# Down products of fourteen of sixteen column groups, in sweeps 2 to 4, by seven half-width products

## The reference

```python
gate = einsum('th,nh->tn', xt, Wg)                # 4096 tokens, 512 -> 4096
up = einsum('th,nh->tn', xt, Wu)
inter = gelu(gate) * up
out = einsum('tn,hn->th', inter, Wd)              # 4096 -> 512
x = layernorm(x + out)
```

## Time and profile before

| | |
|---|---|
| median of 3 runs | 2691.85 us (2691.76 to 2693.28) |
| the profiled execution, its own time | 2691.47 us |
| its span, first to last instruction | 2689.7 us |
| PE busy | 98% of the span |
| PE weight loads | 80% |
| DVE, ACT, POOL busy | 58%, 41%, 31% |
| mean granted TensorE clock | 0.993 of full speed |

### The profile page before, as it was taken

One profiled execution on the slowest core, in us unless ns is written; L12 is line 12 of the kernel. 1 busy time (PEld: TensorE's weight loads), 2 busy tenths in 40 slices (PEclk: granted clock), 3 DMA queues, 4 the chain that ended last, 5 costly groups with the idle time before them and its releaser, 6 DMA issues.

```text
span 2689.7 us, 37714 instructions
## 1 busy us (share of the span) xinstructions
PE 2629.1 (98%) x13314; PEld 2147.7 (80%) x13314; DVE 1555.4 (58%) x3224; ACT 1103.2 (41%) x2518; POOL 824.0 (31%) x992
## 2 busy tenths in 40 slices
PE   7999999999789999999999999999999999999998
PEld 6787887778468888888888888888888888888886
DVE  5677777777789888876333333633333363333334
ACT  4666666666644544443222222322222232222221
POOL 1444444443634343434111111321111132111112
PEclk9999999999899999999999999999999999999999
DMA  8676876778465655565444333554344345433441
GB/s 247 182 186 172 220 210 172 189 193 228 110 245 212 226 213 208 196 264 232 169 174 188 162 141 142 207 206 172 142 185 167 141 158 229 169 141 141 180 172 48
DMA packets 143085, 493.52 MB, mean 183 GB/s; under 512 B 11568, under 2 KB 48560, under 8 KB 118320
## 3 DMA queue, kind: packets, MB, share of 16 engines
q1 hardware_dynamic: 142896, 491.11, 53.0%
HBM read 356.84 MB, written 134.22 MB: 183 GB/s over the span
## 4 chain that ended last, share of the span: by engine, by line
PE 71%; DVE 1%; DMA 1%; issue 1%; ACT 0%; POOL 0%; SPq 0%; POOLq 0%; DVEq 0%; ACTq 0%
PE bank L1034 23%; PE bank L1035 23%; PE bank L1036 23%; PE bank L451 0%; DMA scale<-down_scales 0%; DMA x1T_scratch<-x_late 0%; DVE bstats L1482 0%; PE bank L437 0%; DVE acc L1425 0%; ACT probs L559 0%; PE bank L461 0%; PE bank L418 0%; ACT bx_h L1165 0%; DVE bits L1385 0%; DVE y L704 0%
## 5 line engine op out<-in xcount | busy, mean ns | idle before, releaser
L1644 POOL TENSOR_TENSOR inter_l<-hid,inter_h 128x512 fp32r<-128x512 f32 x256 | 337.6, 1319 | 1362.0 <-ACT inter_h L1165 1362.0
L1425 DVE TENSOR_TENSOR acc<-acc,bank 128x512 f32<-128x512 f32 x512 | 349.9, 684 | 332.4 <-PE bank L1036 322.9
L1034 PE MATMUL bank<-wd,inter_h 128*128 128x512 f32 x1024 | 399.7, 390 | 6.3 <-DVE acc L1425 5.3
L1036 PE MATMUL bank<-wd,inter_l 128*128 128x512 f32 x1024 | 398.9, 390 | 0.0
L1035 PE MATMUL bank<-wd,inter_h 128*128 128x512 f32 x1024 | 398.9, 390 | 0.0
L739 POOL TENSOR_SCALAR probs<-probs,row_inv 128x128 f32<-128x128 f32 (+3 forms) x512 | 263.0, 533 | 366.2 <-DVE row_inv L660 366.2
L1444 DVE TENSOR_TENSOR hid<-hid,bank 128x512 f32<-128x512 f32 x192 | 131.8, 686 | 396.6 <-PE bank L1036 395.0
L1034 PE MATMUL bank<-bx_h,wg 128*128 128x512 f32 x896 | 349.3, 390 | 1.0 <-ACT u_g L1165 1.0
L1036 PE MATMUL bank<-bx_h,wg 128*128 128x512 f32 x896 | 349.1, 390 | 0.0
L1035 PE MATMUL bank<-bx_l,wg 128*128 128x512 f32 x896 | 349.0, 390 | 0.0
L1034 PE MATMUL bank<-bx_h,wu 128*128 128x512 f32 x896 | 348.6, 389 | 0.0
(11 more groups left out here) (139 smaller groups left out, 4355.2 us busy)
## 6 DMA issues: line engine op xcount, KB each, us to landing
wg<-w_scratch SPq DMA_DIRECT2D x48, 1792.0 KB, 8.9
wu<-w_scratch SPq DMA_DIRECT2D x48, 1792.0 KB, 12.8
wd<-w_scratch SPq DMA_DIRECT2D x48, 1024.0 KB, 4.9
q_st<-qk_scratch SPq DMA_DIRECT2D x128, 256.0 KB, 5.1
k_st<-qk_scratch SPq DMA_DIRECT2D x128, 256.0 KB, 6.9
...
```

The lines of the kernel that those rows point to most:

```text
L1034: pe.matmul(out, a(0), b(0), start=start, stop=False, skip_group_check=True)
L1036: return pe.matmul(out, a(1), b(0), start=False, stop=stop, skip_group_check=True)
L1425: dve.tensor_tensor(a, a, d_bank[n % 2][:, :], ALU.add).then_inc(d_added, 1)
L1644: pool.tensor_tensor(inter[1][:, m, t, :], hid[:, 2 * m + t, :], f32(inter[0][:, m, t, :]), ALU.subtract).then_inc(inter_split, 1)
```

## The change

In the 42 quads with j >= 16 and 0 < j % 16 < 15 (`seven(j)`) the down matrix is also taken by seven products. One factor is `inter` (its 2 x 2 tiles and sums of them), the other the 256 x 512 down weights as 2 x 2 blocks of 128 x 256. Each of the seven products is for 512 tokens and 256 outputs, and is issued as two *steps* (half of the tokens each, numbers 0 to 6 and 7 to 13), a step being six matmuls of 128x256: 14 x 6 = 84 matmuls of 256 columns for 48 of 512. A step's result stays in its bank as an addend of later steps of the same parity, and DVE adds each to `acc` (`add_step`, 14 in a quad for 8).

What the seven products need beside that: DVE makes two sums and two differences of `hid` (`hidden_sums`, 4 ops of 128x512), ACT and POOL split seven operands where they split four, and four sums of the down weights (`t_sum`) are needed in high and low parts. These are made once, in sweep 1, in turns 1 to 14: POOL makes four sums of 128x256 at the start of its turn (`sums_of_down`), ACT rounds them at the end of its turn (128x1024), POOL takes the low part at the end of its own (128x1024), and SP stores 1024 KB in `t_scratch` at the start of its next turn. In turn 1 POOL's sums also wait until the last tiles of the attention half are stored, since `t_sum` lies over their memory. In sweeps 2 to 4 SP loads seven slots of 256 KB for each such quad, each as its last reader is done, for one load of 1024 KB.

In the first quad of a sweep and the last, and in the whole of sweep 1, the down products are as before. The diff, cut to what matters (`down`, `load_w` and the waits are otherwise only renumbered):

```diff
+ADD_TO = ((0, 0), (0, 0), (0, 1), (1, 1), (1, 1), (0, 1), (1, 0))
+FRESH = (0, 1, 3)
+WEIGHT_OF = {0: (0, 0), 1: (1, 0), 5: (1, 1)}
+SUM_OF = {2: 0, 3: 1, 4: 2, 6: 3}
...
+    t_sum = plan("t_sum", [P, 4, HALF], F32, over="spare0")
+    t_parts = plan("t_parts", [P, 4, 2, HALF], F32R, over="out_stage")
+    s1_parts = [plan(f"s1_{n}", [P, TILE], F32R, over="w32_d", skip=4 * TILE * i) for i, n in enumerate("hl")]
+    s4_low = plan("s4_l", [P, TILE], F32R, over="wd_0", skip=3 * 8 * HALF)
+    hid_sum = plan("hid_sum", [P, 2, TILE], F32, over="w_sum_g")
+    b_slot = [plan(f"b_slot{i}", [P, 2, HALF], F32R, over="wd_1" if i < 4 else "wd_0", skip=i % 4 * 8 * HALF)
+              for i in range(7)]
...
+    def seven(j):
+        return j >= NG and 0 < j % NG < NG - 1
...
+        def store_t(j):
+            sp.wait_ge(t_split, j)
+            sp.dma_start(t_dram[j], f32(t_parts[:, :, :, :])).then_inc(t_stored, 16)
...
+        def load_operands(j, a, b):
+            for i in range(a, b):
+                if seven(j - 1):
+                    sp.wait_ge(down_done, place_free(j, i))
+                else:
+                    sp.wait_ge(down_done, steps(j - 1) if i < 4 else steps(j))
+                if i in WEIGHT_OF:
+                    m, c = WEIGHT_OF[i]
+                    sp.wait_ge(w_stored[2][j % 2], 16 * (NG // 2))
+                    src = w_dram[j % NG, :, 2 * GU_W:].rearrange("p (l m h) -> p l m h", l=2, m=2)[
+                        :, :, m, c * HALF:(c + 1) * HALF]
+                else:
+                    sp.wait_ge(t_stored, 16 * (NG - 2))
+                    src = t_dram[j % NG, :, SUM_OF[i], :, :]
+                sp.dma_start(f32(b_slot[i][:, :, :]), src).then_inc(b_loaded[i], 16)
...
+                if 1 < j < NG:
+                    store_t(j - 1)
...
+        def step(j, n):
+            i, half = n % 7, n // 7
+            if half == 0:
+                pe.wait_ge(inter_split, parts(j) + i + 1)
+                pe.wait_ge(b_loaded[i], 16 * (sevens(j) + 1))
+            pe.wait_ge(d_added, steps(j) + n - 1)
+            for q in range(2):
+                tokens = slice((2 * half + q) * P, (2 * half + q + 1) * P)
+                last = three(d_bank[n % 2][:, q * HALF:(q + 1) * HALF], lambda l: part(i, l)[:, tokens],
+                             lambda l: b_slot[i][:, l, :], i in FRESH and q == 0, True)
+            last.then_inc(down_done, 1)
...
+        def with_steps(j):
+            p1(j, "g")
+            p1(j, "u")
+            step(j - 1, 0)
+            p6(j, "g")
+            step(j - 1, 1)
+            p2(j, "g")
+            step(j - 1, 2)
...
+            p3(j, "u")
+            step(j - 1, 12)
+            step(j - 1, 13)
...
+        def operand_high(j, i):
+            if i in (0, 1, 6):
+                act.wait_ge(hid_done, chain(j, *{0: (0, 0), 1: (1, 0), 6: (1, 1)}[i]))
+            else:
+                act.wait_ge(hid_summed, 4 * sevens(j) + {3: 1, 2: 2, 4: 3, 5: 4}[i])
+            act.wait_ge(down_done, place_free(j, i))
+            copy(part(i, 0), operand(i)).then_inc(inter_high, 1)
...
+        def sums_of_down_high(j):
+            act.wait_ge(t_summed, 4 * j)
+            if j > 1:
+                act.wait_ge(t_stored, 16 * (j - 1))
+            copy(t_parts[:, :, 0, :], t_sum[:, :, :]).then_inc(t_high, 1)
...
+        def with_operands(j, last):
+            st = j // NG
+            seed(j, "g")
+            seed(j, "u")
+            operand_high(j - 1, 2)
+            operand_high(j - 1, 3)
+            take_u2(j, "g")
+            operand_high(j - 1, 4)
+            operand_high(j - 1, 5)
+            gelu(j, 0, 0)
+            operand_high(j - 1, 6)
+            take_u2(j, "u")
+            take_u3(j, "g")
+            if last:
+                x_part(st + 1, 0, x_next)
+                x_part(st + 1, 1, x_next)
+            take_u3(j, "u")
+            if last:
+                x_part(st + 1, 2, x_next)
+            gelu(j, 1, 1)
...
+                if 0 < j < NG - 1:
+                    sums_of_down_high(j)
...
+        def add_step(j, n):
+            i, half = n % 7, n // 7
+            t, c = ADD_TO[i]
+            dve.wait_ge(down_done, steps(j) + n + 1)
+            if i in (1, 4):
+                dve.wait_ge(d_added, steps(j) + n)
+            a = acc[:, SUB * t + 2 * half:SUB * t + 2 * half + 2, c * HALF:(c + 1) * HALF]
+            dve.tensor_tensor(a, a, d_bank[n % 2][:, :].rearrange("p (a n) -> p a n", a=2), ALU.add).then_inc(d_added, 1)
...
+        def hidden_sums(j, first):
+            a11, a21, a12, a22 = (hid[:, n, :] for n in range(4))
+            s1, s2 = hid_sum[:, 0, :], hid_sum[:, 1, :]
+            done = 4 * sevens(j)
+            if first:
+                dve.wait_ge(hid_done, chain(j, 0, 1))
+                if seven(j - 1):
+                    dve.wait_ge(inter_split, parts(j - 1) + 4)
+                dve.tensor_tensor(s1, a21, a22, ALU.add).then_inc(hid_summed, 1)
+                dve.wait_ge(hid_summed, done + 1)
+                dve.tensor_tensor(s2, s1, a11, ALU.subtract).then_inc(hid_summed, 1)
+            else:
+                dve.tensor_tensor(a21, a11, a21, ALU.subtract).then_inc(hid_summed, 1)
+                dve.wait_ge(inter_split, parts(j) + 2)
+                dve.wait_ge(hid_summed, done + 2)
+                dve.tensor_tensor(a12, a12, s2, ALU.subtract).then_inc(hid_summed, 1)
...
+        def with_steps(j, last):
+            st = j // NG
+            for n in range(4):
+                add_step(j - 1, n)
+            times_up(j, 0, 0)
+            add_step(j - 1, 4)
+            if last:
+                dve.wait_ge(inter_split, parts(j - 1) + 4)
+                sum_x(st + 1, x_next)
+            add_step(j - 1, 5)
+            make_c22(j, "g")
...
+        def operand_low(j, i):
+            pool.wait_ge(inter_high, parts(j) + i + 1)
+            pool.tensor_tensor(part(i, 1), operand(i), f32(part(i, 0)), ALU.subtract).then_inc(inter_split, 1)
...
+        def sums_of_down(j):
+            pool.wait_ge(w_made, 2 * UNITS * (j + 1))
+            if j == 1:
+                pool.wait_ge(ends.x1_stored, BATCH * 16 + STORED_CREDIT)
+                for stored in ends.x1T_stored:
+                    pool.wait_ge(stored, BATCH * TT // 2 * 16 + STORED_CREDIT)
+            else:
+                pool.wait_ge(t_split, j - 1)
+            w = w32[2]
+            b11, b12, b21, b22 = (w[:, m, c * HALF:(c + 1) * HALF] for m in range(2) for c in range(2))
+            t2, t1, t3, t4 = (t_sum[:, n, :] for n in range(4))
+            pool.tensor_tensor(t1, b12, b11, ALU.subtract).then_inc(t_summed, 1)
+            pool.tensor_tensor(t3, b22, b12, ALU.subtract).then_inc(t_summed, 1)
+            pool.wait_ge(t_summed, 4 * j - 3)
+            pool.tensor_tensor(t2, b22, t1, ALU.subtract).then_inc(t_summed, 1)
+            pool.wait_ge(t_summed, 4 * j - 1)
+            pool.tensor_tensor(t4, b21, t2, ALU.subtract).then_inc(t_summed, 1)
...
+        def sums_of_down_low(j):
+            pool.wait_ge(t_high, j)
+            pool.tensor_tensor(t_parts[:, :, 1, :], t_sum[:, :, :], f32(t_parts[:, :, 0, :]),
+                               ALU.subtract).then_inc(t_split, 1)
...
+                if 0 < j < NG - 1:
+                    sums_of_down(j)
                 if prep:
                     sum_w(j + 1, 0)```

**PE, sweeps 2 to 4**, around p6g and p2g of a quad. Before (`wd` and `inter` are a down product, `wg` and `bx` a gate product):

```order
L1034 MATMUL bank<-wd_107,inter_h 128x512
L1035 MATMUL bank<-wd_107,inter_h 128x512
L1036 MATMUL bank<-wd_107,inter_l 128x512
L1034 MATMUL bank<-wd_107,inter_h 128x512
L1035 MATMUL bank<-wd_107,inter_h 128x512
L1036 MATMUL bank<-wd_107,inter_l 128x512
L1034 MATMUL bank<-bx_h,wg_100 128x512
L1035 MATMUL bank<-bx_l,wg_100 128x512
L1036 MATMUL bank<-bx_h,wg_100 128x512
```

169 lines of the change are left out of this document (150 added, 19 removed).

## The result

The changed kernel takes 2726.2 us (2725.9 to 2728.5) for 2691.9 (2691.8 to 2693.3) before, ratio 1.0129, 95% interval 1.0117 to 1.0142: **slower by 34.4 us**, where +17 was forecast (2709, range 2672 to 2732, which holds it). The sign and the stretches in which time is lost came out as forecast; two sizes did not, and both missed to the same side.

What follows compares the result with a forecast made beforehand. PE's matmul count times pitch was taken as the bound, with DVE nearly full in sweep 1. Sweep 1 +46, 42 quads -37 and last quads +8 gave +17: 2709 us, range 2672 to 2732 (the forecast's own 2697 to 2722).

Steps and rivals of the forecast that it cites:

- The cost of sweep 1: Sweep 1: a chain through ACT, DVE and POOL makes the period 33.1 against PE's 29.9; 46 us lost.
- the gain of the 42 quads: Sweeps 2 to 4: 84 narrow matmuls for 48 wide save PE 0.88 us per quad, 37 us in all.
- the last quads: Ends of sweeps 2 and 3: DVE also makes the next tokens, so PE waits; 8 us lost (4 to 12).
- both neighbours: Outcomes beside forecast and between: mild chain (2655 to 2682), chance 0.20; longer chain or costly steps (over 2722), 0.15.
- The forecast's layout with the hold 0.14 shorter than the op: Sweep 1: POOL and DVE alternate, each holding the other for about its duration less 0.14; period 33.1.
- 35.0: Sweep 1, rival: holds last the whole op, period 35.0, 22 us more; chance 0.15 shared with other outcomes over 2722.
- The rival of a clock that falls behind the new gaps: Sweep 1: PE's clock falls to 1.2 GHz behind gaps of about 2.5; 2731; 0.15 shared with others over 2722.
- before d3 or through u3: Sweep 1: PE feels the chain through add 1, needed by d3 at 15 us into the turn, and u3.
- I take none, since a step follows 512 or 256 columns: 42 quads: no loss for waits at a step's start; at 0.08 for each of 588 steps, 47 us.
- The rival with waits that show: 42 quads: 0.05 on each of 588 steps; 2738, or 2701 with the mild chain; 0.15 shared with others over 2722.
- Everything else taken at nothing: 42 quads: added DVE, ACT and POOL work, adds and slot loads cost nothing under PE's 29 us.
- Turn 1: Sweep 1: S, the end of ACT's rounded gate sums, at 794.4; the next at 829.0, 12.8 late.

Runs made afterwards that it cites:

- half_low: Changed kernel with POOL's low part of the new sums at half size from turn 2 on; 2714.0 us, ratio 1.0079.
- moved3: Changed kernel, POOL's new sums moved a turn earlier, ACT's rounding and POOL's low part at once behind them; 2688.5 us, ratio 0.9984.
- no_low: Changed kernel without POOL's low part of the new sums in turns 2 to 14; 2690.5 us, ratio 0.9989.
- halves: Kernel before, each down product of sweeps 2 to 4 as two halves of 256 output columns; 2728.7 us, ratio 1.0133.
- early_sums: Changed kernel, three of four sums of the next sweep's tokens made one each in earlier turns; 2719.4 us, ratio 1.0099.
- all3: Changed kernel with `moved3`, `early_sums` and PE's steps issued two by two; 2681.2 us, ratio 0.9957.
- no_sums: Changed kernel without making the sums of the down weights in sweep 1, plain weights loaded instead; 2682.5 us, ratio 0.9954.
- moved: Changed kernel, POOL's sums and low part moved to where POOL stood idle, ACT rounding behind its second split_high; 2715.1 us, ratio 1.0073.
- moved2: `moved` with ACT's rounding of the new sums back at the end of its turn; 2694.1 us, ratio 1.0005.
- all4: `all3` with PE's steps standing singly again in turns 31 and 47; 2676.8 us, ratio 0.9940.

## Why the prediction was right and where it was wrong

The cost of sweep 1 and its cause were right; what failed is the gain of the 42 quads, forecast at 37 us and measured at 22.7. That accounts for 14 of the 17 us between +17 and +34, and the last quads for 3. The range of 2672 to 2732 holds the result only because it was drawn wide enough to take in most of both neighbours; the forecast's own range, 2697 to 2722, does not.

**Sweep 1: right, in mechanism and size.** The period was laid out as 33.1 and is 33.06; the loss as 46 and is 45.6. The rounded gate sums end at 829.21 in turn 2, where 829.0 was laid out. That a chain closes from one rounded gate sum to the next through ACT, DVE and POOL, and that an added op on it costs its own length, is shown by `half_low` (1.09 off the turn for 1.10 off the op), and that it is place and not amount by `moved3` (the same ops, 29.92). The holds between POOL and DVE are shown as well: 0.7 of them vanish in `no_low`, and 1.9 us of DVE's time in `moved3`. The Trainium skill ("SBUF — State Buffer", Who interferes with whom) has the port pair that DVE and POOL share as an exclusive lock. The traces agree that the loser is held (3.63 for 1.28), and that DVE's adds from PSUM are not (1.27 for two). The forecast's layout with the hold 0.14 shorter than the op was the one that met the period; 35.0 falls. The rival of a clock that falls behind the new gaps is half right: it falls, in four of thirteen turns, and costs nothing, since PE's next wait is shorter by as much. One place was laid out wrongly: PE feels the chain before d0, through the add behind the stretched scaling, and not before d3 or through u3. That did not change the period, which is set on the other engines.

**The seven-product turn: the sign right, the size wrong.** This is the step that failed. That "the step from 512 to 256 columns costs nothing extra" was read from the earlier trace rows and holds. "I take none, since a step follows 512 or 256 columns" looked only at the way into a step. The way out was put at nothing without being looked at: a product behind a step takes 1.39 for 1.36, 13 times a turn, 0.39 us, less 0.04 for steps of 0.71 where 0.714 was used. So 0.54 is gained per quad for 0.88, 22.7 for 37. The rival with waits that show had 0.05 on each of 588 steps and so the wrong cause; `halves` has 0.023 of the 0.03 without any steps. The trace of before held a hint of it, a few rows below those that were used: behind 256-column matmuls and one 512-column matmul with a wait of 0.16, the six from 22.62 take until 24.01, 1.39, and the next six until 25.37, 1.36. The wait ahead of them could have made this as well, so the row asked for a test rather than gave a price.

```profile
22.62 0.39 PE L418 MATMUL bank<-x_l,w_h 128*128 128x512 f32 x1
...
24.01 0.39 PE L418 MATMUL bank<-x_l,w_h 128*128 128x512 f32 x1
...
25.37 0.39 PE L418 MATMUL bank<-x_l,w_h 128*128 128x512 f32 x1
```

**The last quads: right, at the upper end.** 8 was forecast (4 to 12), 10.8 measured. PE waits four times for `add_step` around turn 31, by 0.58, 1.74, 0.97 and 0.97; the longest were laid out as 2.2 and 0.7. These waits make 4.3 us, and 4.0 was laid out; but the two turns are 5.4 longer, since a wait costs PE more than its own length (the turn behind is 1.23 longer for a wait of 0.97). That is the difference of 8 and 10.8. The cause, DVE's token sums in the same turn, is shown by `early_sums`.

**Everything else taken at nothing** was nothing: from 1330 us on PE waited 8.5 us for `add_step`, 0.5 for `add_down` and 0.2 for a load of weights, and for no operand, no slot and no sum of `hid`.

**Turn 1: right.** The changed kernel stands 9.9 us for u_g there, as laid out (S put at 794.4 and found at 794.71, PE going on at 795.25), and the granted clock is 0.52 in the ten us around it, the lower level, 1.2 GHz, and 0.97 in the next ten:

```profile
795.25 0.80 PE L1124 MATMUL bank<-bx_h,wg 128*128 128x512 f32 x1 [9.86 <-ACT u_g L1300]
```

```profile
790.00:800.00 10.00, 4.75 (x11) 3.80 (x12) 5.22 (x7) 4.07 (x7) 7.27 (x7) 0.52 0.86 331
800.00:810.00 10.00, 9.04 (x38) 7.07 (x38) 8.37 (x14) 5.76 (x10) 4.27 (x5) 0.97 0.63 230
```

The start of turn 2 moves with the attention half ahead of it, from 813.6 in `halves` to 820.2 in `all3`, so it is counted from the start of turn 1's d0. From there it is 36.4 us in the kernel before, 35.5 in `halves` and 37.2 in `no_sums`, which do nothing new in turn 1, and 41.2 in the changed kernel: turn 1 costs about 4.9. In `moved`, `moved2`, `moved3`, `all3` and `all4` it is 40.3, about 4 more than before: PE no longer waits for u_g, but 8.1 us for DVE's add where it waited 4.8 before. With turns 2 and 3 that makes some 7 us that `moved3` and `all4` still lose there; what makes that add late was not put to a test.
